# Scattered rows in other buffers, stores and loads at other points, and another order of the small steps between attention and experts

## The reference

```python
h = layernorm(x) * (1 + ca) + sa
q, k, v = h @ wq + bq, h @ wk + bk, h @ wv + bv      # 16 heads of 16
scores = einsum(q, k) * dmask                        # gamma_h ** (n - m) for n >= m, no softmax
ret = scores @ v; norm = group norm of ret per (token, head) * gn_w + gn_b
x = x + ga * ((silu(h @ wg + bg) * norm) @ wo + bo)
h = layernorm(x) * (1 + cb) + sb
top2 of h @ gate_kernel (8 experts), softmax over the two
x = x + gb * sum over the two experts of weight * (silu(h @ w0[e]) * (h @ w1[e])) @ wo[e]
```

## Time and profile before

| | |
|---|---|
| median of 3 runs | 436.94 us (436.1 to 725.89) |
| profiled execution, own time | 437.0 us |
| its span, first to last instruction | 435.1 us |
| mean granted PE clock | 0.929 |
| busy: PE, DVE, POOL, ACT | 379.4, 262.3, 226.8, 168.9 us |
| DMA | 50.62 MB, mean 116 GB/s |

### The profile page before, as it was taken

The page is one execution under the profiler, slowest core; times in us unless marked ns, Lnnn a source line. Parts: engine busy times, 40 slices in busy tenths (PEclk is TensorE's granted clock), DMA queues, the critical chain, the costliest instruction groups (busy, mean ns, idle before and its releaser), DMA issues.

```text
span 435.1 us, 11442 instructions
## 1 busy us (share of the span) xinstructions
PE 379.4 (87%) x3888; PEld 279.4 (64%) x3889; DVE 262.3 (60%) x723; ACT 168.9 (39%) x258; POOL 226.8 (52%) x172
## 2 busy tenths in 40 slices
PE   1996799889978957979989949999999999999990
PEld 1754557566755734746645528888888888888860
DVE  4166735755774754666384526777777777777740
ACT  2250443626153402132311125555555555555530
POOL 3021151443863472427253745777777777777751
PEclk9997969989998976689998969999999999999996
DMA  7836025407741466218746742333344333333222
GB/s 242 242 101 243 3 104 189 112 24 256 246 104 63 158 201 192 77 49 275 100 80 209 206 128 43 72 82 77 84 76 80 73 73 73 73 73 73 49 25 24
DMA packets 35390, 50.62 MB, mean 116 GB/s; under 512 B 4996, under 2 KB 22296, under 8 KB 35352
## 3 DMA queue, kind: packets, MB, share of 16 engines
q1 hardware_dynamic: 25112, 36.17, 29.2%
q0 software_dynamic: 8176, 13.65, 14.4%
q10 hardware_dynamic: 2064, 0.28, 0.5%
HBM read 31.93 MB, written 18.16 MB: 115 GB/s over the span
## 4 chain that ended last, share of the span: by engine, by line
PE 76%; issue 6%; DMA 6%; DVE 5%; ACT 3%; POOL 2%; POOLq 1%; SPq 0%; ACTq 0%; DVEq 0%
PE ps L1654 14%; PE ps L1369 8%; PE ps L1635 6%; PE ps L1634 6%; PE ps L1638 6%; PE ps L1625 5%; PE ps L1377 4%; PE ps L1646 3%; PE ps L1488 3%; PE ps L1396 3%; PE ps L1462 3%; PE ps L1430 3%; DMA out_dram<-wg_s,qd 3%; PE ps L1556 2%; PE ps L1506 2%
## 5 line engine op out<-in xcount | busy, mean ns | idle before, releaser
L621 POOL TENSOR_TENSOR w_lo<-we,w_hi 128x1024 fp32r<-128x1024 f32 x30 | 74.1, 2471 | 27.4 <-ACT w_hi L806 27.4
L1654 PE MATMUL ps<-we,qeo 128*128 x312 | 75.5, 385 | 1.3 <-ACT qeo L791 0.8
L1654 PEld LDWEIGHTS ps<-we,qeo 128*128 128x128 f32 x312 | 57.6, 190 | 19.4 <-issue 12.2
L791 ACT COPY qeo<-ps 128x512 f32<-128x512 f32 x39 | 22.9, 586 | 114.8 <-PE ps L1646 114.8
L631 POOL DMA_INDIRECT out_dram<-wg_s,qd x30 | 46.8, 1560 | 32.9 <-DMA out_dram<-wg_s,qd 14.7
L1276 DVE TENSOR_TENSOR w_halves<-we,w_halves 128x1024 fp32r<-128x1024 f32 x30 | 36.8, 1225 | 6.9 <-ACT w_halves L806 6.7
L1625 PE MATMUL ps<-we,xn 128*128 x72 | 38.2, 658 | 0.7 <-issue 0.7
L1248 DVE CAST rT_halves<-ps 128x256 fp32r<-128x256 f32 x30 | 12.7, 425 | 40.3 <-PE ps L1556 40.3
L806 ACT CAST w_hi<-we 128x1024 fp32r x30 | 31.6, 1053 | 0.2 <-issue 0.2
L806 ACT CAST w_halves<-we 128x1024 fp32r x30 | 31.4, 1048 | 0.1
L1634 PE MATMUL ps<-w_halves,rT_halves 128*128 128x512 f32 x60 | 29.3, 488 | 0.0
(11 more groups left out here) (235 smaller groups left out, 746.7 us busy)
## 6 DMA issues: line engine op xcount, KB each, us to landing
rowbuf<-routed SPq DMA_DIRECT2D x39, 260.5 KB, 2.9
we<-in_ffn_w_kernel_dram SPq DMA_DIRECT2D x16, 512.0 KB, 4.7
we<-in_ffn_wo_kernel_dram SPq DMA_DIRECT2D x8, 512.0 KB, 6.2
routed<-z SPq DMA_DIRECT2D x9, 260.5 KB, 3.8
xs<-in_attn_x_dram SPq DMA_DIRECT2D x4, 512.0 KB, 13.9
out_dram<-xs SPq DMA_DIRECT2D x4, 512.0 KB, 4.0
we<-in_wmod_dram SPq DMA_DIRECT2D x1, 1536.0 KB, 7.3
sbcb<-gsc_dram SPq DMA_DIRECT2D x4, 256.0 KB, 3.9
```

Source lines behind the costliest of these rows:

```text
L621: g.tensor_tensor(w_lo[1], expert_up(e, 1), w_hi[1].bitcast(F32), ALU.subtract)\
L1654: last = mm(down_ps, eit[s % 2][:, k, :], weights(e, 2 * FT * F + k * D, D), start=k == 0, stop=k == KF - 1)
```

## The change

1. Homes of the rows: batch 0 in the eighth expert's room, batches 1 and 3 in `h2_own`, batch 2 over the first rows of x (with 40 floats of padding ahead of x, so that only batches 0 and 1 of x are overlaid). Small constants lose their own buffers and borrow others.
2. SP: `store_x` of batches 0 and 1 goes from behind `attention_out` to the head of the pass after (behind the first q projection); that of batch 2 goes into the experts' row loads, behind the last values. The eighth expert's weights are loaded in pass 3 beside the seventh's, after batch 0's scatter. The waits of `fill_gb` and `second_normed` follow the new homes.
3. PSUM ring and orders in pass 3: on DVE `tiles_before(0)` goes ahead of the statistics of `attention_out` (now `attention_stats`), `tile_columns(0)` and `table_rows(0)` go behind the first and second `masks`; on PE `fold(0)` goes behind `values(b, 0)`.
4. Between attention and experts: `rank(2)` goes behind `average` and `average_dev` of batch 3, in the ring too.
5. Experts' steps: POOL does `modulate` of batch 3 in two halves behind `add_rows` 0 and 1 (the second half waits for `row_ready`) and no longer behind 2; the scatters of batch 3 go behind `add_rows` 2 and 3, no longer 4 and 5. Round 1 of the table is made about one step earlier: `tiles_before(1)` inside `dve_step` 5, `tile_columns(1)` behind it, `table_rows(1)` behind step 6.

```diff
@@ tail_items
-        if b >= 2:
-            items.append((b - 2, "rank", "dve"))
+        ranks = [(b - 2, "rank", "dve")] if b >= 2 else []
         if b >= 1:
-            items += [(b - 1, n, "dve") for n in ("gn", "wo01", "wo23")]
+            group, rows = (b - 1, "gn", "dve"), [(b - 1, n, "dve") for n in ("wo01", "wo23")]
+            items += ([group] + ranks if b == B else ranks + [group]) + rows
...
-            items += [(b, "firsts", "dve"), (b, "fold", "dve")]
+            items.append((b, "firsts", "dve"))
...
-            items += [(b - 1, "h2T0", "act"), (b - 1, "h2T1", "act"), (b - 1, "logits", "dve")]
+            items += [(b - 1, "h2T0", "act"), (b - 1, "h2T1", "act")]
+        if b == B - 1:
+            items.append((b, "fold", "dve"))
+        if b >= 1:
+            items.append((b - 1, "logits", "dve"))
@@ homes
-        xs = sb("xs", [P, B * NC, D])
+        xrows = sb("xrows", [P, XPAD + B * NC * D])
+        xs = xrows[:, XPAD:].rearrange("p (i d) -> p i d", d=D)
-        h2 = [h2_own[:, :, :], h2_we, h2_own[:, :, :], h2_xs]
+        h2 = [h2_we, h2_own[:, :, :], h2_xs, h2_own[:, :, :]]
@@ fill_gb, and the same waits in ACT's second_normed
-                if b == B - 1:
-                    sp.wait_ge(x2_out, 16 * (B - 1))
-                    sp.wait_ge(h2n_ready, NC * (B - 1))
-                elif b >= 2:
-                    sp.wait_ge(scattered, SCATTERS * (b - 1))
+                if b == 2:
+                    sp.wait_ge(x2_out, 16 * b)
+                    sp.wait_ge(h2n_ready, NC * b)
+                elif b == B - 1:
+                    sp.wait_ge(scattered, SCATTERS * 2)
@@ SP, passes
                 sp.wait_ge(front.full, front.filled(b, "q0"))
+                if b >= 2:
+                    store_x(b - 2, x2_out)
                 if b == B - 1:
                     sp.wait_ge(gb_out, 16)
                 load_expert(2 * b)
                 sp.wait_ge(front.full, front.filled(b, "k0"))
-                if b < B - 1:
-                    load_expert(2 * b + 1)
+                if b == B - 1:
+                    sp.wait_ge(scattered, SCATTERS)
+                load_expert(2 * b + 1)
                 if p >= 0:
-                    store_x(p, x2_out)
...
-            sp.wait_ge(scattered, SCATTERS * (B - 2))
-            load_expert(E - 1)
@@ SP, experts' rows
             for i in range(EARLY):
                 load_rows(i, i)
                 if i == 1:
+                    sp.wait_ge(pv_done, SETS * B)
+                    store_x(B - 2, x2_out)
                     sp.wait_ge(h2_ready, B - 1)
                     load_sbcb(B - 1)
@@ POOL, experts' steps
-                if i == 2:
-                    modulate(B - 1)
-                if i in (4, 5):
-                    scatter(B - 1, (2 * i - 8, 2 * i - 7))
+                if i == 0:
+                    modulate_scale(B - 1)
+                if i == 1:
+                    pool.wait_ge(row_ready, B)
+                    modulate_shift(B - 1)
+                if i in (2, 3):
+                    scatter(B - 1, (2 * i - 4, 2 * i - 3))
@@ DVE, pass 3
                 if last:
                     tiles_before(0)
+                if p >= 0:
+                    attention_stats(p)
...
-                if last:
-                    tile_columns(0)
...
                 masks(b, 0)
                 gates(b, 0)
                 if last:
-                    table_rows(0)
+                    tile_columns(0)
                 else:
                     gates(b, 1)
...
                 masks(b, 1)
+                if last:
+                    table_rows(0)
@@ DVE, experts' steps
-                dve_step(i, i, hidden_made=i == 2)
+                dve_step(i, i, hidden_made=i == 2, between=(lambda: tiles_before(1)) if i == 5 else None)
...
                 elif i == 5:
-                    tiles_before(1)
+                    tile_columns(1)
                 elif i == 6:
-                    tile_columns(1)
-                elif i == 7:
                     table_rows(1)
@@ PE
                 from_states(b)
-                if final:
-                    fold(0)
-                else:
+                if not final:
                     project_gate(b, 1)
...
                 values(b, 0)
+                if final:
+                    fold(0)
...
             project_gate(b, 1)
-            rank(b - 1)
             average(b)
             turn_rows(0, 0)
             average_dev(b)
+            rank(b - 1)
...
-            pe_step(5, 5, between=lambda: counts(1))
-            pe_step(6, 6, between=lambda: firsts(1))
-            pe_step(7, 7, between=lambda: fold(1))
+            pe_step(5, 5, between=lambda: counts(1), before_down=lambda: firsts(1))
+            pe_step(6, 6, before_down=lambda: fold(1))
+            pe_step(7, 7)
```

More of the change, by code:

```diff
@@ L49 @@
 WE = FT * F * 2 + KF * D
+XPAD = 40
+assert XPAD + 2 * NC * D >= NC * ROW
 CH = 64
@@ L152, in adaln_block @@
         bv_bc, bo_bc = sb("bv_bc", [P, D]), sb("bo_bc", [P, D])
-        gam_bc = sb("gam_bc", [P, H])
         ident, tri, ones, blkavg = (sb(n, [P, P]) for n in ("ident", "tri", "ones", "blkavg"))
-        hmask = sb("hmask", [P, HPT])
         par, bqp, blk32 = sb("par", [P, 2]), sb("bqp", [P, 2, FT]), sb("blk32", [P, 2 * DH])
-        erow_i, erow = sb("erow_i", [P, E], I32), sb("erow", [P, E])
-        ebase_i, ebase = sb("ebase_i", [P, E], I32), sb("ebase", [P, E])
+        erow, ebase = sb("erow", [P, E]), sb("ebase", [P, E])
         tokid = sb("tokid", [P, B * NC], I32)
@@ L177, in adaln_block @@
         mv1 = sb("mv1", [P, B * NC, 2])
-        ve1, nm1, rs1, nmr1 = (sb(n, [P, B * NC]) for n in ("ve1", "nm1", "rs1", "nmr1"))
+        ve1, nm1 = (sb(n, [P, B * NC]) for n in ("ve1", "nm1"))
+        rs1, nmr1 = ve1, nm1
         xn = sb("xn", [P, NC, D])
@@ L203, in adaln_block @@
         h2_we = we[:, E - 1, 0:NC * ROW].rearrange("p (t r) -> p t r", t=NC)
-        h2_xs = xs[:, :, :].rearrange("p i d -> p (i d)")[:, 0:NC * ROW].rearrange("p (t r) -> p t r", t=NC)
-        h2 = [h2_own[:, :, :], h2_we, h2_own[:, :, :], h2_xs]
+        h2_xs = xrows[:, 0:NC * ROW].rearrange("p (t r) -> p t r", t=NC)
+        h2 = [h2_we, h2_own[:, :, :], h2_xs, h2_own[:, :, :]]
         h2T = [hT, hT, qd, hT]
@@ L219, in adaln_block @@
                              sb("cmb", [P, 2, NC, E]))
+        gam_bc, hmask = cmb[:, 0, 0:2, :].rearrange("p t e -> p (t e)"), oh[:, 0, 0, :]
+        erow_i, ebase_i = oh[:, 0, 1, :].bitcast(I32), oh[:, 0, 2, :].bitcast(I32)
         vd, vt, pk = sb("vd", [P, NC]), sb("vt", [P, NC]), sb("pk", [P, 2, NC])
@@ L456, in _ @@
             sp.wait_ge(front.full, front.filled(B - 1, "v23"))
+            sp.wait_ge(scattered, SCATTERS * (B - 2))
             sp.wait_ge(tab_ready, 2)
@@ L551, in decay_q, with modulate_scale @@
                                 ALU.mult).then_inc(qd_ready, 1)
-            def modulate(b):
+            def modulate_scale(b):
                 hv = h2[b][:, :, 0:D]
@@ L560, in modulate, with modulate_shift @@
                                 ALU.mult).then_inc(h2m_ready, 1)
+            def modulate_shift(b):
+                hv = h2[b][:, :, 0:D]
                 pool.wait_ge(h2m_ready, b + 1)
@@ L612, in _ @@
                 if p >= 0:
-                    modulate(p)
+                    modulate_scale(p)
+                    modulate_shift(p)
             group_power(B - 1)
@@ L735, in second_normed @@
                 act.wait_ge(shift2, b + 1)
[L736 to L739, removed]
+                if b == 2:
+                    act.wait_ge(x2_out, 16 * b)
+                elif b == B - 1:
+                    act.wait_ge(scattered, SCATTERS * 2)
                 for t in range(NC):
@@ L1048, in attention_out, with attention_stats @@
                     v.tensor_tensor(xv, xv, att, ALU.add).then_inc(tail.drained["dve"], 1)
+            def attention_stats(b):
                 wait(dve, tail.drains(b, "wo23"))
@@ L1277, in weights_lo, with dve_step @@
                     .then_inc(w_lo_ready[0], 1)
-            def dve_step(i, s, hidden_made=False):
+            def dve_step(i, s, hidden_made=False, between=None):
                 const = isinstance(i, int)
@@ L1282, in dve_step @@
                     hidden(i - 1, s - 1)
+                if between is not None:
+                    between()
                 if not (const and not 0 <= i - 2 < N_TILES):
@@ L1308, in _ @@
             attention_out(b)
+            attention_stats(b)
             attention_moments(b)
```

## The result

| | before | after |
|---|---|---|
| median | 436.52 us (4 runs, 433.81 to 725.89) | 411.23 us (4 runs, 410.1 to 414.83) |
| profiled execution, own time | 437.0 us | 410.27 us |
| its span | 435.1 us | 408.4 us |
| mean granted PE clock | 0.929 | 0.954 |

The ratio is 0.9454, 95% interval 0.9366 to 0.9543: 5.5% faster. Ratios rest on the fast runs of each kernel alone, medians on all its runs, the one of 725.89 us included, so the two need not agree to the last us. The prediction was 419.1 us, range 411 to 427. The median lies at the range's very edge: the direction held, the size was 18 us where 25 were measured. In the profiled executions it is 26.7 us, and these can be placed.

A forecast was written before the change was run, and what follows sets the result against it. PE was taken as the bound, busy 87% of the span, leaving its idle time and low-clock stretches to win: 437.0 - 5.2 (pass 3) - 1.8 (rank) - 10.9 (experts' steps) = 419.1 us, range 411 to 427.

The forecast's parts named there:

- Homes, stores, gate rows in passes 1 and 2: Passes 1 and 2: the moved transfers save nothing that shows; taken as 0, bounds -1 and +1 us.
- The wait for instructions in pass 3: Pass 3: with less DMA traffic PE's 4.18 us "issue" wait shrinks to 3.2; gain 1.0 us, bounds 0 and 1.9.
- DVE order in pass 3: Pass 3: earlier `tiles_before(0)` gains 1.2 us at `state_parts`; masks ahead of `tile_columns(0)` gain 2.5 us.
- Clock in pass 3: Pass 3: with less idle time some half-clock work runs at full clock; gain 0.5 us, bounds 0 and 2.8.
- Rank behind the averages: Between attention and experts: waits of `average` and POOL's power go; gain 1.8 us, bounds 0.5 and 3.2.
- The steps: Experts' steps 4 to 9: 12.9 us of waits and slow clock won, less 2.0 us for a new wait; gain 10.9.
- The 2.0 us lost at `added_ok`: Experts' steps: `take_rows(6)` on DVE waits for `add_rows(3)` behind four scatters; loss 2.0 us, bounds 0 and 3.5.
- 1: Pass 3: the stall only moves, instructions as late as now, the masks' 2.5 us come back; 423 us, chance 0.17.
- 2: Experts' steps: adds 3 and 4 land in 10 us behind scatters, 6.6 us lost; 426 us, chance 0.10.
- 4: Experts' steps: every add from 2 to 6 lands in 10 us, kernel slower; 448 us, chance 0.04.
- 3: Experts' steps: the VectorE-GpSimd lock moves along with `modulate`'s halves, indices 2.3 us late; 421.5 us, chance 0.07.
- 5: More than summed: short wait for instructions and full clock through pass 3 and step 0; 414 us, chance 0.09.

The follow-up runs named there:

- e1: Kernel before with only the stores of x moved, gate rows coming earlier with them: 427.8 us against 432.74, ratio 0.9835.
- e6: Changed kernel with four of the eight pad stores behind the row load of tile 8: 408.84 us, ratio 0.9384.
- e10: Changed kernel with the orders of pass 3 (DVE, PE's fold and the ring) back as before: 413.65 us, ratio 0.9445.
- e12: The changed kernel unedited, measured again: 411.42 us against 437.76 for the kernel before, ratio 0.9448.
- e5: Changed kernel with stores of batches 0 and 1 back behind the output projection of passes 1 and 2, gate rows behind them: 419.18 us, ratio 0.9563.
- e3: Kernel before with only the orders of pass 3 changed: 437.81 us against 432.74, no verdict.
- e4: Kernel before with only rank of batch 2 moved behind the averages, on PE and in the ring: 431.32 us against 432.74.
- e2: Kernel before with only the order inside the experts' steps changed: 424.85 us against 432.74, ratio 0.9744.
- e8: Changed kernel with modulate of batch 3 whole behind add 2, as before the change: 417.45 us, ratio 0.9623.
- e11: Changed kernel with only the gate rows of batches 0 and 1 back behind the output projection: 417.96 us, ratio 0.9541.

## Why the prediction was right, and where it was too small

*Homes, stores, gate rows in passes 1 and 2:* taken at 0, bounds -1 and +1. This is the step that failed. It measured 4.2 us in v1 to v2, 2.3 of idle time and 1.8 by the clock. The eight kernels with stores and gate rows moved (e1, after, e6 to e10, e12) took 33.77 to 34.12, the five with the stores behind the output projection 37.94 to 41.99. I had one of the waits before me, the 2.24 us, and read it as what a wait for instructions costs with empty queues. It was itself made by the moved transfers (e1 removes it, e5 brings it back). The queues were full ahead of it and not during it: their share is 0.49 in the 2.2 us before and 0.05 while PE waits. How a transfer that is over still lengthens the wait, no run shows. v2 to v3 gave 1.5 us in the profiles, but its column runs from 37.17 to 41.71 without order, so nothing is shown there.

*The wait for instructions in pass 3, 1.0:* not seen. It was 4.63 us after for 4.18 before, and 1.34 to 4.63 over all fourteen kernels, in no relation to stores, gate rows, scatter or weights. Its cause stays open. Shown is only that PE waits for nothing that the profile records, and that an instruction packet arrives inside the wait; that it is a wait for instructions is my reading.

*DVE order in pass 3, 1.2 + 2.5:* right. Both waits went, and e10 brings both back with 3.4 us or more. Alone (e3) they gave 1.1 us of pass 3, beside a new 3.13 us wait for "issue" that began ahead of the weights' load.

*Clock in pass 3, 0.5, and the sum of pass 3, 5.2:* the sum measured 5.7, and that it fits is partly luck. Idle time fell by 2.75 us, where the terms for waits add up to 4.7, and the clock rose from 0.76 to 0.88, which took 3.0 us off the busy time, above the upper bound of 2.8. The clock was the mis-sized term that made up for the 1.0 that didn't come.

*Rank behind the averages, 1.8:* 1.3, of which 1.1 are idle time; e4's 1.9 are mostly clock. POOL's power starts with the variance, as said.

*The steps, 10.9:* 10.05 from rank to step 9, by e2 all from this item. Inside the sum two terms were wrong and nearly cancelled. The 2.0 us lost at `added_ok` didn't happen, since POOL's sequencer doesn't wait for its engine's scatters. And the pads, said to be through by 20 us after step 4, were issued until 17.5 and the load behind them landed at 24: 2.79 us at tile 8, a load I had passed over in writing only of tile 9. e6 removes the wait.

*Rivals:* 1 came by half: the wait for "issue" is as long as before, but the 2.5 us of `masks` didn't come back. 2 and 4 didn't come: add 5 starts 5.98 us after add 4 (227.54 and 221.56), and PE never waits for an add. The steady loop is as it was (173.29 us behind step 9 before, 173.00 after). The other sign of being wrong, growing landings, shows a little: over the early steps an add lands in 4.7 us in the median before and 5.1 after, the longest 9.2 and 8.2. 3 is there as a mechanism (2.23 for about 0.3 us at 197.26) without a price, and e8 prices it where it was: 3.1 us. 5 came nearest in the number, and part of its clock in pass 3 came, but its short wait didn't; what brought the number there is the term that I had at nothing.

*Chance:* 3.9 us of the profiled difference lies before v1 and is none of the change's. That leaves 22.8 us. The medians differ by 25.3 us, and in e12's comparison by 26.3; in which stretches the 2.5 to 3.5 us between lie, these profiles don't show.

## What to carry to other kernels

A transfer that nobody waits for can still cost PE time, in waits and in the clock behind them. Here the gate rows cost nothing where they were issued beside the v and output projections (64 to 72 us after, PE busy throughout at full clock), and 3.3 us beside the many small matmuls of scores and states. Count the issue time of a queue of small jobs that stands ahead of a load. Where VectorE and GpSimd hold each other up, place the long operation where the other works from PSUM or waits anyway, and look again after every shift. Cut profiles at the same operations, compare stretches over several kernels, and read idle time and clock of each apart: this kernel's time spreads by 5 to 10 us on one chip, and gains of 2 to 4 us were plain in a stretch and invisible in the time.

## What the runs showed of the hardware that I had not expected

- PE's wait for "issue" at one and the same matmul of pass 3 was anything from 1.34 to 4.63 us over kernels that differ nowhere near it.
- GpSimd's sequencer runs ahead of its engine: it passed the semaphore step behind four scatters before the fourth had begun (copy at 212.58, scatter at 213.26).
- Gate-row broadcasts kept the DMA engines 0.54 busy at 79 GB/s (e11, 78 to 84 us).
- A store whose DRAM row comes from a register costs SP 9.82 / 8 = 1.2 us of issue, about 0.34 of it the issue itself.
- The clock that PE lost behind waits weighed about as much as the waits: in v1 to v2, e11 lost 1.2 us in idle time and 2.1 by the clock.
